# Decoder kernel, layer 0: who issues the rows of maxima, where the raw mask lands, and the order of SyncE's queue

## The chip, the cores and the metric

The kernel runs on one core of one Trainium2 chip. The metric is the device time of one execution in microseconds (us). The engines are TensorE (PE), VectorE (DVE), ScalarE (ACT), GpSimd (POOL) and SyncE (SP); SP computes nothing and issues DMAs. DMAs that an engine issues stand in the profile as SPq or ACTq.

## The reference, cut to what matters

A decoder of four layers, each of self attention, cross attention over a context and a feed-forward part, on x of 4 batches x 256 tokens x 128 features; the context has 4 x 512 tokens. The change lies in layer 0:

```
x = x + L0_attn(layernorm(x))                  # self attention, 16 half heads of 8 features, pairs combined
x = x + L0_xattn(ctx, ctx, layernorm(x), mask) # cross attention, 16 heads of 8 features
x = x + L0_ffn(layernorm(x))                   # 8 experts and a shared one

# L0_attn
probs = softmax(einsum('bhtd,bhsd->bhts', rope(q), rope(k)))     # 256 x 256 per half head
diff  = probs[:, :, 0] - lam * probs[:, :, 1]
attn  = einsum('bhts,bhsd->bhtd', diff, v); attn *= rsqrt(mean(attn*attn) + 1e-5) * (1 - LAMBDA_INIT)
# L0_xattn
energy = einsum('nqhd,nkhd->nhqk', q, k)
energy = where(mask == 0, -1e20, energy)                         # mask: 4 x 1 x 256 x 512, int32
out    = einsum('nhql,nlhd->nqhd', softmax(energy / sqrt(128)), v) @ W_fc.T + b_fc
```

## The kernel before, in words

The kernel is written out by hand: each engine has one program (`tensor_program`, `scalar_program`, `vector_program`, `gpsimd_program`, `sync_program`), run in its own order, and the engines meet only at semaphores. Nothing is reordered by a scheduler.

The two attentions of layer 0 run as one sequence of slots `t` (line 1188). In self attention (A0) a batch has 8 slots, one per pair of heads; cross attention (X0) has 16 slots per batch and begins at slot 36, so that its slot 0 is the same as A0's slot 36. In a slot TensorE makes one pair's scores (L545 for A0, L550 for X0), VectorE takes their maxima (L1666, L1672), and 12 slots later (20 in X0) TensorE makes the transposed scores again with the maximum subtracted (L531), ScalarE takes the exponentials (L1242) and TensorE sums them with the values (L585). Each batch is closed some 21 slots after it began: VectorE and GpSimd normalise it (`l0a_rms`, `power`, L2426), TensorE turns and projects it (L509, L517), and VectorE, GpSimd, TensorE and ScalarE make its X0 queries (`turn_norm`, L478; `split_queries`, L2439 to L2442).

The operands of the scores are stacks: `q_stack` (per batch), `self_stack` (A0's keys) and `ctx_stack` (the context's keys). A float32 operand is split in three bf16 parts, which a DMA writes to DRAM (`write_parts`, L2596, to `q_scr`, `k_scr`, `c_scr`), and which two DMAs (one for each parity of heads) read back into 48 rows of a stack (`fill_rows`, L2602). Further rows of a stack hold ones or zeros (`fill_row`, L2618), and three rows of `q_stack` hold the parts of the row maxima, which come from `mT` (`max_rows`, L2644). TensorE waits for these at the first exponential slot of a batch (`d_maxrow`, L557), for a batch's queries at its first score slot (`d_qfill`, L564) and for the context's stack at X0's slot 0 (`d_cfill`, L680).

SP issues nearly all DMAs, in the order of `sync_program`; an instruction there that waits holds up all behind it. In the first stage the order is: the stacks of batch 0; the transposed context `ctxT` (1 MB); batch 1; the raw mask (2 MB, into `ctx_stack`, which is free then); batch 2; maxima of batch 0; batch 3; the context's parts (12 writes); maxima of batch 1; the bulk loads `rows`, `vaug`, `keep`; maxima of batch 2; then, once GpSimd has turned the raw mask into `far_q` (L2565, `far_done`), the rows and parts of `ctx_stack`; X0's queries of batch 0; maxima of batch 3; X0's other queries and its first maxima; the weights of the feed-forward part (`L0f_w`, 4.6 MB).

GpSimd's order (lines 2551 to 2572) is: keys of batches 0 to 2, context pieces 0 and 1, keys of batch 3, context pieces 2 and 3, the mask (8 instructions), and then for each batch the root (L2426) with which it is closed.

Of the kernel before, what the change touches and what calls it, by code (L numbers as in the profile page):

```python
# [23 lines left out]
ALU = mybir.AluOpType  # L24
# [128 lines left out]
CFILL = {X0: 64, X1: 160, X2: 224}  # L153
# [41 lines left out]
def build(nc, d, out, ctx):  # L195
# [98 lines left out]
    mask_raw = ctx_flat[:, 0:4096].bitcast(I32).rearrange("p (t k) -> p t k", t=NT)  # L294
# [165 lines left out]
    def tensor_program():  # L460
# [216 lines left out]
        def cross_slot(use, t, w_out, following, tile=ring):  # L677
            if t == 0:
                pe.wait_ge(d_ones, 128)
                pe.wait_ge(d_cfill, CFILL[use])  # L680
# [531 lines left out]
    def scalar_program():  # L1212
# [67 lines left out]
        def l0a_slot(t):  # L1280
            g, odd = divmod(t - 15, 2)
            if not odd and 0 <= g < 16:
                lift(A0, g, SUM0[A0] + g + 1)
            for b in range(B):
                at = t - close_slot(A0, b)
                if at == 4:
                    turned_close(A0, b)
                if at == 8:
                    turned_norm("L0x", b, qT, scale=RSQRT128)
            if t == 8:  # L1290
                act.wait_ge(lam_sum, 1)
                act.activation(lam[:, 2:4], lam[:, 0:2], ACT.Exp).then_inc(lam_exp, 1)
            if 0 <= t - 12 < 32:
                exps(A0, t - 12)
            if t == 10:
                l0a_values_of(3)

        def cross_slot(use, t, following):
# [3 lines left out]
            for b in range(B):  # L1302
# [1114 lines left out]
    def gpsimd_program():  # L2417
# [145 lines left out]
        pool.wait_ge(d_raw, 16)  # L2563
        for t in range(NT):
            pool.tensor_scalar(far_q[:, t, :], mask_raw[:, t, :], 0, -BIG, ALU.is_equal, ALU.mult).then_inc(far_done, 1)  # L2565
# [25 lines left out]
    def sync_program():  # L2591
# [100 lines left out]
        for b in range(1, B):  # L2692
            max_rows(X0, b)
# [190 lines left out]
```

## Time and profile before

| | us |
|---|---|
| median of 3 runs (lowest, highest) | 1306.96 (1304.37, 1311.36) |
| the profiled execution's own time | 1301.29 |
| its span | 1300.0 |
| busy PE / DVE / ACT / POOL | 1018.1 / 809.3 / 588.7 / 232.9 |
| DMA queue q1 (SP's) | 65.19 MB, 15.7% of 16 engines' span |

The chain that ended last is 55% PE, 27% DVE, 5% DMA. A share over the whole span says little of one stage, so the stretch from 0 to about 200 us, in which the changed code runs, has to be read by itself: where its engines stood still, and what ended that. In the rows, "idle before <- releaser" is in square brackets, and the engine PEld is TensorE's load of weights.

### The profile page before, as it was taken

The page shows a single profiled execution, that of the slowest core. Times are in us where ns is not written, and L with a number is a line of the kernel's source. Part 1 is how long each engine was busy: PE and PEld are TensorE (multiplying, and loading weights), DVE is VectorE, ACT ScalarE, POOL GpSimd, SP SyncE. Part 2 cuts the span into 40 slices and gives each one's busy share as a digit, 9 for nine tenths or more (in the row PEclk, how much of TensorE's full clock was granted, in tenths as well). Part 3 has the DMA queues.
Part 4 walks back from the last instruction along what each step waited for, and adds up shares of the span by engine and source line. Part 5 has one row for each costly group of instructions (what it writes and reads, how often), then busy time and mean ns, then how long its engine had stood idle before and what let it go on. Part 6 is the DMA issues. An engine that isn't in the chain of part 4 may idle for free.

```text
span 1300.0 us, 18604 instructions
## 1 busy us (share of the span) xinstructions
PE 1018.1 (78%) x7025; PEld 543.5 (42%) x7025; DVE 809.3 (62%) x2015; ACT 588.7 (45%) x975; POOL 232.9 (18%) x299
## 2 busy tenths in 40 slices
PE   3375559999899995586766789999856878868999
PEld 2132212333377673344444233466522333336757
DVE  5575476771221646888777785486778878765422
ACT  1054315666424533687673568422203645533342
POOL 3362230000000023376542100000101100110000
PEclk9587657999789997577777699899956889989999
DMA  4663132000000030044102500310100300100000
GB/s 118 201 246 116 41 95 100 2 2 2 1 1 1 1 98 33 4 143 139 59 1 94 178 3 2 86 51 1 42 7 25 124 1 2 33 1 1 1 9 9
DMA packets 47680, 67.42 MB, mean 52 GB/s; under 512 B 4903, under 2 KB 41976, under 8 KB 45896
## 3 DMA queue, kind: packets, MB, share of 16 engines
q1 hardware_dynamic: 46872, 65.19, 15.7%
q10 hardware_dynamic: 720, 1.05, 0.3%
q8 instruction: 56, 0.92, 0.3%
q14 instruction: 32, 0.26, 0.1%
HBM read 46.83 MB, written 19.01 MB: 51 GB/s over the span
## 4 chain that ended last, share of the span: by engine, by line
PE 55%; DVE 27%; DMA 5%; issue 4%; ACT 4%; SPq 2%; POOL 2%; DVEq 0%; ACTq 0%; POOLq 0%
PE ps_s L755 9%; PE ps_e L745 9%; DVE mx L1676 6%; PE ps_v L585 6%; PE ps_e L531 4%; PE ps_s L550 3%; PE ps_e L529 3%; DMA q_scr<-parts 3%; DVE ps_s L1672 2%; PE ps_e L842 2%; PE ps_s L829 2%; DVE work L2154 2%; ACT work L1242 2%; DVE work L2156 2%; DVE xn L1632 1%
## 5 line engine op out<-in xcount | busy, mean ns | idle before, releaser
L1242 ACT ACTIVATE work<-ps_e 128x512 f32<-128x512 f32 x448 | 250.6, 597 | 185.8 <-PE ps_e L531 180.6
L550 PE MATMUL ps_s<-ctx_stack,q_stack 49*128 49x512 bf16 x384 | 130.9, 466 | 52.5 <-DVE mx L1676 37.5
L1676 DVE TENSOR_REDUCE mx<-ps_s 128x2 f32<-128x1024 f32 x128 | 153.7, 1221 | 29.2 <-PE ps_s L550 27.8
L2426 POOL TENSOR_TENSOR rstd<-rstd,halves 128x2 f32<-128x2 f32 x52 | 36.7, 706 | 751.2 <-DVE rstd L1619 751.1
L1335 ACT ACTIVATE work<-ps_s,keep 128x512 f32<-128x512 f32 x136 | 93.1, 687 | 146.2 <-PE ps_s L755 143.2
L531 PE MATMUL ps_e<-q_stack,ctx_stack 52*128 52x256 bf16 x768 | 149.8, 293 | 12.0 <-DMA q_stack<-mT 4.4
L585 PE MATMUL ps_v<-work,vaug 128*32 128x256 f32 x1536 | 130.0, 414 | 4.6 <-ACT work L1230 4.6
L745 PEld LDWEIGHTS ps_e<-ffn_w,work 128*128 128x128 f32 x960 | 119.2, 198 | 21.0 <-issue 19.9
L755 PE MATMUL ps_s<-xnT,ffn_w 128*128 128x512 f32 x240 | 119.8, 627 | 3.6 <-ACT work L1335 3.6
L745 PE MATMUL ps_e<-ffn_w,work 128*128 128x128 f32 x960 | 121.0, 281 | 0.8 <-DVE x L1870 0.8
L1672 DVE CUSTOM_DVE_ANT_0 ps_s<-ps_s,work 128x512 f32<-128x512 f32 x128 | 85.9, 716 | 56.5 <-PE ps_s L550 56.3
L1880 DVE SCALAR_TENSOR_TENSOR x<-ps_e,gates,x 128x128 f32<-128x128 f32 x128 | 39.0, 346 | 127.0 <-PE ps_e L745 124.0
L531 PEld LDWEIGHTS ps_e<-q_stack,ctx_stack 52*128 52x128 bf16 x768 | 45.0, 96 | 108.2 <-ACT work L1242 50.6
L550 PEld LDWEIGHTS ps_s<-ctx_stack,q_stack 49*128 49x128 bf16 x384 | 29.4, 98 | 81.5 <-DVE mx L1676 51.4
L755 PEld LDWEIGHTS ps_s<-xnT,ffn_w 128*128 128x128 f32 x240 | 42.6, 199 | 45.2 <-issue 25.5
L529 PE MATMUL ps_e<-work,ident_b 128*128 128x512 bf16 x128 | 52.4, 409 | 5.4 <-issue 5.4
L1666 DVE TENSOR_REDUCE mx<-ps_s 128x4 f32<-128x1024 f32 x32 | 38.1, 1218 | 22.1 <-PE ps_s L545 21.8
L585 PEld LDWEIGHTS ps_v<-work,vaug 128*32 128x32 f32 x1536 | 31.6, 111 | 47.9 <-issue 35.5
L2482 POOL TENSOR_TENSOR work<-work 128x1536 f32<-128x1536 f32 x14 | 48.0, 3439 | 12.8 <-ACT work L1473 12.8
L531 PE MATMUL ps_e<-q_stack,self_stack 52*128 52x256 bf16 x128 | 23.4, 333 | 30.4 <-DMA q_stack<-mT 29.6
L1707 DVE RECIPROCAL rsum<-ps_s 128x8 f32<-128x8 f32 x48 | 9.7, 202 | 60.0 <-PE ps_s L501 60.0
L1222 ACT ACTIVATE xnT<-ps_m 128x256 f32<-128x256 f32 x36 | 13.8, 383 | 68.1 <-PE ps_m L478 67.3
(358 smaller groups left out, 1748.2 us busy)
## 6 DMA issues: line engine op xcount, KB each, us to landing
q_stack<-q_scr SPq DMA_DIRECT2D x40, 192.0 KB
ctx_stack<-c_scr SPq DMA_DIRECT2D x4, 1536.0 KB
ffn_w<-in_L0f_w SPq DMA_DIRECT2D x1, 4608.0 KB, 15.2
q_scr<-parts SPq DMA_DIRECT2D x20, 192.0 KB, 2.1
ffn_w<-in_L1f_w SPq DMA_DIRECT2D x1, 3456.0 KB, 14.0
self_stack<-k_scr SPq DMA_DIRECT2D x16, 192.0 KB
ctx_stack<-kx_scr SPq DMA_DIRECT2D x2, 1536.0 KB
ffn_w<-in_L3f_w SPq DMA_DIRECT2D x1, 3072.0 KB, 13.2
```

The lines of the kernel that those rows point to most:

```text
L529: pe.matmul(bank[name], ident_b[:], far_k[:, b, k:k + 2, :].rearrange("p k q -> p (k q)"), start=True, stop=False, skip_group_check=True)
L531: m = pe.matmul(bank[name][:, half * S:(half + 1) * S], stack[p0:p0 + K_EXP, pair, b * nk + k * P:b * nk + (k + 1) * P], q_stack[p0:p0 + K ...
L550: return pe.matmul(ps_s[i][:, parity, :], q_stack[p0:p0 + K_SCORE, b, pair, part * P:(part + 1) * P], ctx_stack[p0:p0 + K_SCORE, pair, b * ...
L585: m = pe.matmul(ps_v[j * COLS:(j + 1) * COLS, 0:S], values(b * nkt + k, g % 4 * GROUP + j), pt[:, j % 2, k % 2, :], start=(k == 0), stop=( ...
L745: m = pe.matmul(bank[name][:, i * P:(i + 1) * P], hid[:, j, (t0 + i) * P:(t0 + i + 1) * P], w2(e, j), start=(j == 0), stop=(j == FJ - 1))
L755: pe.matmul(bank[name], w1_of(st, e, j), xnT[:, g * 512:(g + 1) * 512], start=True, stop=True).then_inc(UPS[st], 1)
L1242: act.activation(pt[:, parity, :, :].rearrange("p k q -> p (k q)"), bank[f"e{parity}"], ACT.Exp).then_inc(exped, 1)
L1335: act.activation(hid_unit(st, u)[:, j, :], bank[f"h{n % 2}"], ACT.Gelu_apprx_tanh, bias=b1).then_inc(HIDS[st], 1)
L1672: m = dve.tensor_tensor_reduce(ps_s[i][:, parity, :], ps_s[i][:, parity, :], far_q[:, b * TPB + part, :], 1.0, -3e38, ALU.add, ALU.max, mx ...
L1676: m = dve.tensor_reduce(mx[:, b, :, pair, part], ps_s[i][:], AX, ALU.max, negate=True)
L1880: m = dve.scalar_tensor_tensor(x[:, t, :], bank[f"e{(n - 1) % 2}"][:, i * P:(i + 1) * P], scalar_of(e, t), x[:, t, :], ALU.mult, ALU.add)
L2482: pool.tensor_tensor(c, c, l1_s[:, HALVES[n], :], ALU.add).then_inc(added, 1)
```

## The change

Six edits, in layer 0's two attentions alone.

- `max_rows` for A0 and X0 is issued by ScalarE, from a new function in `scalar_program`, in A0's slots 11, 19, 27, 35 and in X0's slots 18, 34, 50, 66, ahead of the slot's exponentials. Later stages keep SP's.
- The raw mask is loaded in two halves, into `ffn_w` and into `work`, and no longer into `ctx_stack`.
- The rows of ones of `ctx_stack` are written at the start (on `d_cfill`, whose counts go up by 32).
- SP writes the parts of batches 1 and 2 and fills both stacks ahead of `ctxT` and of the mask.
- `ctx_stack` is filled right behind the context's parts and `rows`, ahead of `keep` and `vaug`; that fill waits for `d_cwrite` alone and no longer for `far_done`.
- X0's queries of all four batches stand in a row, without maxima between them.

```
-        pool.wait_ge(d_raw, 16)
+        pool.wait_ge(d_raw, 32)
...
+        def max_rows(use, b):
+            act.wait_ge(max_T, BATCH0[use] + b + 1)
+            for parity in range(2):
+                p0 = parity * SLOT + ROW_MAX
+                act.dma_start(q_stack[p0:p0 + 3, b, :, :].rearrange("s h (q t) -> s (h q) t", q=TPB),
+                              mT[parity * 48:(parity + 1) * 48, b, :]).then_inc(d_maxrow[b], 16)
...
+            if t in (11, 19, 27, 35):
+                max_rows(A0, (t - 11) // 8)
...
+            if use == X0 and t in (18, 34, 50, 66):
+                max_rows(X0, (t - 18) // 16)
...
+        fill_row(ctx_stack, one_row, 3, ROW_MAX, d_cfill)
         lam_at = ROW_AT["lq1"][0]
         self_attention_inputs(A0, 0)
+        sp.dma_start(rows[:, lam_at:], ...).then_inc(d_lam, 16)
+        for b in (1, 2):
+            queries(A0, b)
+            keys(A0, b)
+        for b in (1, 2):
+            fill_queries(A0, b)
+            fill_self_keys(A0, b)
         sp.dma_start(ctxT, d["ctxT"][:, :]).then_inc(d_ctx, 16)
-        self_attention_inputs(A0, 1)
-        sp.dma_start(rows[:, lam_at:], ...).then_inc(d_lam, 16)
-        sp.dma_start(mask_raw, ...).then_inc(d_raw, 16)
-        self_attention_inputs(A0, 2)
-        max_rows(A0, 0)
+        for half in range(2):
+            sp.dma_start(mask_raw[half], mask_tiles[:, 4 * half:4 * half + 4, :]).then_inc(d_raw, 16)
         self_attention_inputs(A0, 3)
         for g in range(4):
             ...
-        max_rows(A0, 1)
         sp.dma_start(rows[:, 0:lam_at], ...).then_inc(d_rows, 16)
+        sp.wait_ge(d_cwrite, 192)
+        fill_context(c_scr, zero_row)
+        sp.dma_start(keep[:, P:KEEP_N], ...).then_inc(d_keep, 16)
         sp.dma_start(vaug_pad[:, 0:NC * VA], ...).then_inc(d_vload, 16)
-        sp.dma_start(keep[:, P:KEEP_N], ...).then_inc(d_keep, 16)
         ...
-        max_rows(A0, 2)
+        for b in range(B):
+            cross_inputs(X0, b)
         sp.wait_ge(far_done, NT)
-        sp.wait_ge(d_cwrite, 192)
-        fill_row(ctx_stack, one_row, 3, ROW_MAX, d_ones)
-        fill_context(c_scr, zero_row)
-        cross_inputs(X0, 0)
-        max_rows(A0, 3)
-        for b in range(1, B):
-            cross_inputs(X0, b)
-        max_rows(X0, 0)
         sp.wait_ge(x_done, X_AT[A0, B - 1])
         sp.dma_start(ffn_w[:, 0:FFN_N], d["L0f_w"][:, :]).then_inc(d_w, 16)
-        for b in range(1, B):
-            max_rows(X0, b)
```

SP, from the filling of batch 0's stacks to the transposed context; before (`write_parts` is L2596, `fill_rows` L2602, `in_ctxT` the context, `in_mask_L0` the raw mask):

```order
L2602 DMA q_stack<-q_scr 48x1x2048 x2
L2602 DMA self_stack<-k_scr 48x8x256 x2
L2663 DMA work<-in_ctxT 128x2048
L2596 DMA q_scr<-parts 128x3x256
L2596 DMA q_scr<-parts 128x2x256
L2596 DMA q_scr<-parts 128x256
```

SP, the same place of the changed kernel, from the last write of batch 2's keys on (there these functions are L2608 and L2614):

```order
L2608 DMA k_scr<-work 128x256
L2614 DMA q_stack<-q_scr 48x1x2048 x2
L2614 DMA self_stack<-k_scr 48x8x256 x2
L2614 DMA q_stack<-q_scr 48x1x2048 x2
L2614 DMA self_stack<-k_scr 48x8x256 x2
L2683 DMA work<-in_ctxT 128x2048
L2686 DMA ffn_w<-in_mask_L0 128x4x512
L2686 DMA work<-in_mask_L0 128x4x512
```

The context stood behind four fills, those of batch 0; now it stands behind twelve, and behind the 12 writes of batches 1 and 2.

SP, from the context's last write to the first of X0's queries; before (`in_rows01` holds the zeros and ones):

```order
L2596 DMA c_scr<-ffn_w 128x512
L2644 DMA q_stack<-mT 3x16x128 x2
L2674 DMA rows<-in_rows 128x2689
L2675 DMA vaug<-in_v_aug 128x2304
L2676 DMA keep<-in_keep 128x2664
L2677 DMA masku8<-in_mask_keys 16x128
L2678 DMA b2<-in_b2_L0 9x128
L2679 DMA b2<-in_b2_L3 8x128
L2644 DMA q_stack<-mT 3x16x128 x2
L2618 DMA ctx_stack<-in_rows01 3x8x2048 x2
L2602 DMA ctx_stack<-c_scr 48x1x16384 x2
L2618 DMA ctx_stack<-in_rows01 1x8x2048 x2
```

SP, the same place of the changed kernel:

```order
L2608 DMA c_scr<-ffn_w 128x512
L2691 DMA rows<-in_rows 128x2689
L2614 DMA ctx_stack<-c_scr 48x1x16384 x2
L2630 DMA ctx_stack<-in_rows01 1x8x2048 x2
L2694 DMA keep<-in_keep 128x2664
L2695 DMA vaug<-in_v_aug 128x2304
L2696 DMA masku8<-in_mask_keys 16x128
L2697 DMA b2<-in_b2_L0 9x128
L2698 DMA b2<-in_b2_L3 8x128
L2608 DMA q_scr<-parts 128x3x256
```

The fill of `ctx_stack` now stands ahead of `keep` and `vaug`, which X0's queries still follow; no rows of maxima stand between.

ScalarE around A0's slot 27 in the changed kernel (exponentials L1243, sums out of `ps_v` L1231, the new rows of maxima L1259; the queue of before has the same rows without the DMA):

```order
L1243 ACTIVATE work<-ps_e0 128x512
L1243 ACTIVATE work<-ps_e1 128x512
L1231 ACTIVATE work<-ps_v 128x256
L1259 DMA q_stack<-mT 3x16x128 x2
L1243 ACTIVATE work<-ps_e0 128x512
L1243 ACTIVATE work<-ps_e1 128x512
```

The two DMAs stand between a lift and the exponentials of their slot, which they hold up.

## Rows read from the trace of the kernel before

**Rows 1.** Windows: us, busy (x) of PE, PEld, DVE, ACT, POOL; PEclk, DMA share, GB/s

```profile
100.00:120.00 20.00, 14.78 (x155) 6.84 (x147) 16.32 (x49) 12.32 (x26) 7.56 (x10) 0.90 0.42 129
120.00:140.00 20.00, 0.00 (x0) 0.00 (x0) 0.82 (x4) 0.00 (x1) 0.62 (x2) 0.53 0.24 83
```

**Rows 2.** Chain of waits, 100 to 145 us: start, us, what

```profile
108.88 25.00 DMA q_scr<-parts
133.89 0.79 SPq L2602
...
136.31 4.17 DMA q_stack<-mT
```

**Rows 3.** Timeline of TensorE: start, us, line, operation, [idle before <- releaser]

```profile
48.49 1.04 PE L545 MATMUL ps_s<-self_stack,q_stack 49*128 49x256 bf16 x8 [6.13 <-DMA self_stack<-k_scr]
...
64.01 0.39 PE L531 MATMUL ps_e<-q_stack,self_stack 52*128 52x256 bf16 x1 [6.39 <-DMA q_stack<-mT]
...
119.17 0.41 PE L501 MATMUL ps_s<-keep,work 128*128 128x128 f32 x2 [0.28 <-ACT work L1230]
...
140.52 0.61 PE L531 MATMUL ps_e<-q_stack,self_stack 52*128 52x256 bf16 x4 [20.95 <-DMA q_stack<-mT]
...
143.55 0.61 PE L550 MATMUL ps_s<-ctx_stack,q_stack 49*128 49x512 bf16 x2
...
194.18 0.58 PE L529 MATMUL ps_e<-work,ident_b 128*128 128x512 bf16 x1 [5.39 <-issue]
```

**Rows 4.** Timeline of SP's queue: start, us of issue, line, DMA, count

```profile
25.84 3.02 SPq L2663 DMA_DIRECT2D work<-in_ctxT  x1
...
30.92 2.49 SPq L2596 DMA_DIRECT2D k_scr<-work  x3
37.42 1.48 SPq L2602 DMA_DIRECT2D q_stack<-q_scr  x2
...
62.78 1.52 SPq L2596 DMA_DIRECT2D k_scr<-work  x3
...
68.43 9.74 SPq L2596 DMA_DIRECT2D c_scr<-ffn_w  x12
...
99.99 1.58 SPq L2602 DMA_DIRECT2D ctx_stack<-c_scr  x2
...
186.45 1.48 SPq L2602 DMA_DIRECT2D q_stack<-q_scr  x2
187.98 1.57 SPq L2644 DMA_DIRECT2D q_stack<-mT  x2
```

**Rows 5.** Windows again, as rows 1

```profile
40.00:44.00 4.00, 1.32 (x10) 0.27 (x8) 3.96 (x5) 0.00 (x0) 3.59 (x5) 0.50 0.38 131
...
82.00:92.00 10.00, 7.07 (x69) 3.06 (x69) 7.12 (x16) 5.03 (x10) 5.03 (x3) 0.83 0.96 367
...
136.00:139.00 3.00, 0.00 (x0) 0.00 (x0) 0.00 (x0) 0.00 (x0) 0.00 (x0) 0.50 0.33 121
```

**Rows 6.** Timeline of GpSimd

```profile
36.36 0.61 POOL L2439 CAST ffn_w<-work 128x512 bf16<-128x512 f32 x1 [5.83 <-DMA work<-in_ctxT]
...
59.54 0.40 POOL L2439 CAST work<-xn 128x256 bf16<-128x256 f32 x1 [15.72 <-DVE xn L1651]
...
61.84 0.61 POOL L2439 CAST ffn_w<-work 128x512 bf16<-128x512 f32 x1
...
69.38 15.95 POOL L2565 TENSOR_SCALAR work<-ctx_stack 128x512 bf16<-128x512 int32 x8
...
90.21 2.92 POOL L2426 TENSOR_TENSOR l0a_ss<-l0a_ss,halves 128x16 f32<-128x16 f32 x1 [4.89 <-DVE l0a_ss L1741]
```

**Rows 7.** DMAs of the page: KB each, median us from issue to landing

```profile
c_scr<-ffn_w SPq DMA_DIRECT2D x4, 384.0 KB, 3.6
```

**Rows 8.** Timelines of VectorE and ScalarE

```profile
187.57 0.21 DVE L1696 COPY mT<-ps_s 96x128 bf16<-96x128 bf16 x1
...
235.79 1.27 ACT L1242 ACTIVATE work<-ps_e 128x512 f32<-128x512 f32 x2 [0.59 <-PE ps_e L531]
```

More of the change, by code:

```diff
@@ L152 @@
 LAST = {A0: 54, X0: 96, X1: 96, X2: 93, "chain": 125}
-CFILL = {X0: 64, X1: 160, X2: 224}
+CFILL = {X0: 96, X1: 192, X2: 256}
 QKV_N = 3 * E + 1
@@ L293, in build @@
     ctx_flat = ctx_stack[:].rearrange("p h t -> p (h t)").bitcast(F32)
-    mask_raw = ctx_flat[:, 0:4096].bitcast(I32).rearrange("p (t k) -> p t k", t=NT)
+    mask_raw = [part.bitcast(I32).rearrange("p (t k) -> p t k", t=NT // 2)
+                for part in (ffn_w[:, ROOM_AT + 3072:ROOM_AT + 5120], wk(4096, 2048))]
     far_q = wk(0, 2048).bitcast(BF16).rearrange("p (t k) -> p t k", t=NT)
@@ L678, in cross_slot @@
             if t == 0:
-                pe.wait_ge(d_ones, 128)
+                pe.wait_ge(d_ones, 96)
                 pe.wait_ge(d_cfill, CFILL[use])
@@ L2562, in gpsimd_program @@
         split_context(3)
-        pool.wait_ge(d_raw, 16)
+        pool.wait_ge(d_raw, 32)
         for t in range(NT):
-            pool.tensor_scalar(far_q[:, t, :], mask_raw[:, t, :], 0, -BIG, ALU.is_equal, ALU.mult).then_inc(far_done, 1)
+            pool.tensor_scalar(far_q[:, t, :], mask_raw[t // 4][:, t % 4, :], 0, -BIG, ALU.is_equal, ALU.mult).then_inc(far_done, 1)
         pool.wait_ge(d_rows, 16)
@@ L2660, in sync_program @@
         fill_row(self_stack, zero_row, 1, ROW_MASK, d_ones)
+        fill_row(ctx_stack, one_row, 3, ROW_MAX, d_cfill)
         lam_at = ROW_AT["lq1"][0]
         self_attention_inputs(A0, 0)
-        sp.dma_start(ctxT, d["ctxT"][:, :]).then_inc(d_ctx, 16)
-        self_attention_inputs(A0, 1)
-        sp.dma_start(rows[:, lam_at:], d["rows"][0:1, lam_at:].broadcast_to([P, ROW_N - lam_at])).then_inc(d_lam, 16)
-        sp.dma_start(mask_raw, d["mask_L0"].rearrange("b o (j p) k -> p (b o j) k", p=P)).then_inc(d_raw, 16)
-        self_attention_inputs(A0, 2)
-        max_rows(A0, 0)
+        sp.dma_start(rows[:, lam_at:], d["rows"][0:1, lam_at:].broadcast_to([P, ROW_N - lam_at])).then_inc(d_lam, 16)
+        for b in (1, 2):
[4 more added lines that the diff above has]
+            fill_self_keys(A0, b)
+        sp.dma_start(ctxT, d["ctxT"][:, :]).then_inc(d_ctx, 16)
+        mask_tiles = d["mask_L0"].rearrange("b o (j p) k -> p (b o j) k", p=P)
+        for half in range(2):
+            sp.dma_start(mask_raw[half], mask_tiles[:, 4 * half:4 * half + 4, :]).then_inc(d_raw, 16)
         self_attention_inputs(A0, 3)
@@ L2672, in sync_program @@
             write_parts(c_scr, KEY_PARTS, c_parts[:, :, g * 512:(g + 1) * 512], g * 512, 512, d_cwrite)
-        max_rows(A0, 1)
         sp.dma_start(rows[:, 0:lam_at], d["rows"][0:1, 0:lam_at].broadcast_to([P, lam_at])).then_inc(d_rows, 16)
+        sp.wait_ge(d_cwrite, 192)
+        fill_context(c_scr, zero_row)
+        sp.dma_start(keep[:, P:KEEP_N], d["keep"][:, P:KEEP_N]).then_inc(d_keep, 16)
         sp.dma_start(vaug_pad[:, 0:NC * VA], d["v_aug"][:, :]).then_inc(d_vload, 16)
-        sp.dma_start(keep[:, P:KEEP_N], d["keep"][:, P:KEEP_N]).then_inc(d_keep, 16)
         sp.dma_start(masku8[:], d["mask_keys"].rearrange("b (j p) -> (b j) p", p=P)).then_inc(d_mk, 16)
```

## The prediction

> **What bounds the kernel now.** I read the windows of 20 us first, to see where TensorE stands still though it has work. From 120 to 140 us every compute engine is idle and the DMA engines are busy for 0.24 of their time [rows 1]. The chain of waits for that stretch says why: a DMA that writes query parts takes 25.00 us to land, SP then issues the fill of `q_stack` at 133.89, and behind it the rows of maxima take 4.17 us [rows 2]. TensorE's timeline gives the price: 20.95 us before its first exponential of A0's batch 3, and X0's first score follows at 143.55 [rows 3]. So the first stage ends in one stall of 21 us, and all that follows in this in-order kernel starts from it. Two more waits on the same kind of rows stand in that timeline: 6.39 us at 64.01 (batch 0) and 5.39 us at 194.18, which is marked "issue" but lies between the issue of X0's rows at 187.98 and their landing [rows 3, 4].
>
> Why did 64 KB take 25 us? They were issued at 108.88 behind the fill of `ctx_stack`, issued from 99.99 on [rows 4]. While only fills are in flight, the share of busy DMA engines is 0.38 or 0.33 [rows 5], which is about 6 of 16. I take it that one fill, whatever its size, runs on six engines, and that what SP issues later waits behind it there. The fill takes about 101.6 to 133.9 = 32.3 us.
>
> **The sum.** It is a new timeline of SP's queue and of what it waits for, against the profiled execution (1301.29 us, 1.29 of them around its span).
>
> *Batches 1 and 2.* A batch's two query fills and two key fills took 37.42 to 48.49 = 11.1 us from first issue to TensorE's use [rows 3, 4], some 9.4 of them on the engines. Before, batch 1's fills stood behind its writes and 1 MB of context. Now `rows` (16.5 KB) takes the context's place, the writes of batch 1 again end at about 33.4 [rows 4], those of batch 2 at about 37, and batch 1's fills land at about 37 + 10 = 47: batch 1 starts 1.5 us sooner. Batch 2's follow 9 us later, at about 56.
>
> *The transposed context* comes behind them: 56 + 2 = 58 us, where GpSimd had it at 36.36 [rows 6]. GpSimd's queue then is: two pieces of context 7.5 us (as 61.84 to 69.38), batch 3's keys 2.3 (59.54 to 61.84), two more pieces 7.5, and the mask 15.95 [rows 6]. That gives 58 + 7.5 + 2.3 + 7.5 + 15.95 = 91.2 us for the root that closes batch 0, which now starts at 90.21 after an idle 4.89 [rows 6]. So the slack in GpSimd's queue is used up, and A0 passes its slot 24 no sooner than before. What TensorE gains at batch 1, and in the wait of 6.39 us at batch 0's maxima, it gives back there. I count 0 for both; their bounds are the 8 us of these two and a loss of as much if the context comes later.
>
> *The context's stack.* Batch 3's keys are split at 58 + 7.5 + 2.3 = 67.8; their three writes take 1.5 to issue [rows 4] and some 2.5 to land (a context write of twice the size takes 3.6 [rows 7]), two fills 1.6: 73.5. The 12 writes of the context take 9.74 us of issue [rows 4] and land 3.6 later: SP's wait ends, and the fill is issued, at about 87, against 99.99. It is 13 us sooner, because neither the mask on GpSimd nor maxima of batch 2 hold it. The data follow the 1.3 MB of `rows`, so say from 88.6, and 32.3 us later, at 120.9, the fill is in. But `keep` and `vaug` now stand behind it: of the 3.9 MB (`rows`, `vaug` and `keep` by their shapes) that moved in the 10 us of 82 to 92 [rows 5] they are 2.5 MB, or 6.5 us. X0's query parts, ready near 108 as now, land at 127.9 (now 133.89), and the fill of `q_stack` takes about 5.4 us (with the rows of maxima behind it 133.89 to 140.52 = 6.6, of which I give these 1.2): X0's first score is at about 133.3. Slots 24 to 35 go as before, since maxima no longer queue at SP, and slot 36's own A0 work (3.0 us between 140.52 and 143.55 [rows 3]) is done before the wait. Gain: 143.55 - 133.3 = **10.2 us**. Bounds: 16.8 if `keep` and `vaug` cost nothing there; 3.7 if they cost twice that.
>
> *X0's rows of maxima, batch 0.* VectorE has them at 187.57 + 0.21 [rows 8] and SP issues at 187.98, so issuing elsewhere saves no wait; but the DMAs land 194.18 - 189.55 = 4.6 us after issue, behind a fill issued at 186.45 [rows 4]. On ScalarE's own queue they need not stand behind it. Bounds 0 and 4.6, I take **2.4 us**.
>
> *ScalarE's issue.* SP pays 1.57 us for two such DMAs [rows 4]. In A0 this delays the exponentials of slots 27 and 35, and the rows share engines with the fill of `ctx_stack`; but between slot 35 (119.2) and 133.3 there are 14 us of stall that hide it. X0's batch 0 finds ScalarE idle. For X0's batches 1 to 3 ScalarE waits only 0.59 us between pairs [rows 8], so each is late by 1.57 - 0.59 = 1.0 us: at most 3 us where TensorE waits for each, 0 where the two banks take it up; I take **1.5 us** lost. Later in the kernel nothing is touched.
>
> The mask in two halves, the earlier rows of ones and X0's queries in a row I cost at nothing: what they move is covered by the stall. Without that cover the ones (192 KB at the 367 GB/s of [rows 5]) would add 0.5 us before the first projection.
>
> Sum: -10.2 - 2.4 + 1.5 = -11.1: 1290.2 us by the profiled execution. That one lies 5.7 us under the median of the runs shown, 1306.96; by that median it is 1295.9. I predict **1296 us**.
>
> *A rule of the Trainium skill against it.* The page "DMA: Bandwidth & Descriptors" (section "Issuing engines are not separate DMA queues") says that DMAs of SP, ScalarE and GpSimd run on the same 16 engines and interleave, and that issuing from several only saves issue time. By it the 2.4 us fall away, since the issue wait was 0.2 us here. The same page (section "Queues, rings and completion order") lets an engine alternate between the queues by packets, by which the rows would pass most of a fill. No row of this trace shows two busy queues; that is why the term stands at the middle of its bounds.
>
> **Rivals.**
>
> *Larger gain.* The context is in sooner, or `keep` and `vaug` slip in on the ten idle engines and cost the six little. For it: 0.24 of DMA share from 120 to 140 means that the fill's engines end unevenly. The first score is at 126.5, a gain of 16.8 + 2.4 - 1.5 = 17.7: 1289 us by the median. Chance 0.16.
>
> *The stall stays where it is.* `keep` and `vaug` cost 13 us behind the fill instead of 6.5: the score at 139.8, with the other terms a gain of 4.6: 1302. For it: with `rows` they needed 10 us on all engines at a share of 0.96 [rows 5]. Against it: fills leave ten engines free. Chance 0.19.
>
> *The rows of maxima gain nothing on ScalarE's queue.* The issue wait it could save is 187.98 - 187.78 = 0.2 us, and if on the DMA engines the rows still follow the fill of 186.45, they land as now: -10.2 + 1.5 = -8.7: 1298. Chance 0.10. The Trainium skill's section on issuing engines, above, describes this case.
>
> *Slower: the transposed context starves GpSimd.* It waits behind eight fills more, and GpSimd can't go on to batch 3's keys without it. For it: SP's issue already takes 3.02 us where it stands behind four fills [rows 4]. Every us that the context lands after 58 moves batch 3, the 12 writes, the context's stack and A0's slot 24 by one. It decides from 58 + 11 = 69 us on. If eight fills take twice their time, it lands at about 76 + 2: 9 us slower, 1316. Chance 0.13.
>
> **How the numbers follow.** My forecast (gain of 7 to 15) has 0.42. Less than 0.5% (6.5 us) can't be told from no change here. Faster by more: 0.40 of the forecast, 0.06 of the rows that gain nothing, 0.16 of the larger gain, 0.02 of the stall that stays = 0.64. Within: 0.02 + 0.04 + 0.16 + 0.04 = 0.26. Slower by more: 0.01 + 0.09 = 0.10. The range goes from 1284, a gain of 23 (the larger gain and the first stage's 8 us kept in part), to 1307, no gain.
>
> **What would show it.** Right: GpSimd's first context piece starts at 55 to 61 us and its first root (on `l0a_ss`) at 89 to 95 with little idle; `ctx_stack` is filled from 84 to 90; the last part of X0's first queries lands at 125 to 131; TensorE's stall is now ahead of a score (L551), 10 to 15 us long, and ends near 133; the rows of maxima land within 3 us of their issue on ScalarE's queue at X0's slot 20; the stretch from there to the end is as long as before. Wrong: the context after 65 us, the fill of `ctx_stack` after 93, TensorE waiting for rows of maxima in A0 for more than some us, or a new wait behind ScalarE's issue in X0's slots 34, 50 and 66.

## The result: 2.0% slower, and the profile after

| | before | after |
|---|---|---|
| median, us (lowest to highest, runs) | 1305.66 (1298.46 to 1311.36, 4) | 1332.19 (1329.26 to 1334.08, 4) |
| profiled execution's own time | 1301.29 | 1331.33 |
| its span | 1300.0 | 1330.0 |
| TensorE's mean granted clock | 0.848 | 0.829 |

The ratio is 1.0204, with a 95% interval of 1.0149 to 1.0259. The forecast was 1296, its range 1284 to 1307, and 0.10 for slower: wrong in sign.

Where the 30.0 us of span came in, TensorE's timeline shows (start, us, what, [idle before <- releaser]); the columns answer to [rows 3].

```profile
44.13 1.04 PE L546 MATMUL ps_s<-self_stack,q_stack 49*128 49x256 bf16 x8 [4.64 <-DMA self_stack<-k_scr]
...
57.94 0.39 PE L532 MATMUL ps_e<-q_stack,self_stack 52*128 52x256 bf16 x1 [4.92 <-DMA q_stack<-mT]
...
81.49 0.39 PE L532 MATMUL ps_e<-q_stack,self_stack 52*128 52x256 bf16 x1 [4.89 <-DMA q_stack<-mT]
...
130.35 0.39 PE L532 MATMUL ps_e<-q_stack,self_stack 52*128 52x256 bf16 x1 [29.45 <-DMA q_stack<-mT]
...
154.43 0.61 PE L551 MATMUL ps_s<-ctx_stack,q_stack 49*128 49x512 bf16 x2
...
217.82 0.39 PE L532 MATMUL ps_e<-q_stack,ctx_stack 52*128 52x256 bf16 x1 [16.80 <-issue]
...
367.14 1.20 PE L756 MATMUL ps_s<-xnT,ffn_w 128*128 128x512 f32 x1
```

Batch 1 starts 4.4 us sooner (44.13 for 48.49), and batch 0's rows of maxima 6.1 us sooner. Then come two waits that the forecast did not have. The first is 29.45 us at slot 28, for the rows of maxima of A0's batch 2. It swallows the old stall of 20.95 us and more: X0's first score starts at 154.43, 10.9 us later than before, where the forecast had 133.3. The second is 16.80 us at X0's first exponential, where 5.39 stood before; the stretch from X0's first score to that row grew from 50.6 to 63.4 us, so by 12.8. From that row to the first GELU operand of the feed-forward part (L756) it takes 149.32 us, against 150.20 before (194.18 to 344.38). So the stretch up to there is longer by 10.9 + 12.8 - 0.9 = 22.8 us, of 30.0 in all. The other 7.2 lie in code that is the same in both kernels (962.9 us from L756 to the end for 955.6). The eleven experiments below, with that same code, have 958.5 to 967.7 us there, so I take these 7.2 as scatter of the stretch, in which the profile of before was the shortest of all. TensorE's granted clock in it was 0.87 before and 0.85 after. The medians, 26.5 us apart, leave only 3.7 us for it. What makes it scatter, and whether the change has a part in it, was not tested.

The chain of waits (start, us, what) names the first stall as [rows 2] named the old one.

```profile
99.97 0.38 ACT work L1231
100.35 0.38 ACTq L1259
100.77 29.54 DMA q_stack<-mT
...
203.35 14.47 issue
```

ScalarE issues the rows at 99.97, and they take 29.54 us from issue to landing. That is not a wait to issue; it is a transfer of 24 KB in flight. SP's queue (start, us of issue, what) says what was in flight with it; it answers to [rows 4].

```profile
43.30 3.16 SPq L2683 DMA_DIRECT2D work<-in_ctxT  x1
...
67.93 10.13 SPq L2608 DMA_DIRECT2D c_scr<-ffn_w  x12
...
82.22 1.48 SPq L2614 DMA_DIRECT2D ctx_stack<-c_scr  x2
...
85.17 0.44 SPq L2694 DMA_DIRECT2D keep<-in_keep  x1
85.65 0.43 SPq L2695 DMA_DIRECT2D vaug<-in_v_aug  x1
...
136.74 1.71 SPq L2608 DMA_DIRECT2D q_scr<-parts  x3
139.99 1.56 SPq L2614 DMA_DIRECT2D q_stack<-q_scr  x2
...
200.26 0.39 SPq L2703 DMA_DIRECT2D ffn_w<-in_L0f_w  x1
```

The fill of `ctx_stack` goes out at 82.22, 17.8 us sooner than before and so ahead of the rows of batch 2. Right behind it on SP's queue come the bulk loads `keep` (1332 KB) and `vaug` (1152 KB), 85.17 and 85.65. Before, the order of SP's queue kept the fill behind the rows: `max_rows(A0, 2)` at 97.23, then the fill at 99.99 [rows 4]. Likewise `L0f_w` (4608 KB) is issued at 200.26, 0.2 us after X0's rows, while SP before issued it behind them on the same queue (189.59, the rows at 187.98). The two lines of SP's old queue that [rows 4] leaves out:

```profile
97.23 1.47 SPq L2644 DMA_DIRECT2D q_stack<-mT  x2
...
189.59 0.43 SPq L2691 DMA_DIRECT2D ffn_w<-in_L0f_w  x1
```

ScalarE's timeline has the two sets of rows beside them, and one of those in X0's later batches:

```profile
99.97 1.53 ACTq L1259 DMA_DIRECT2D q_stack<-mT  x2
...
200.04 1.50 ACTq L1259 DMA_DIRECT2D q_stack<-mT  x2
...
250.35 1.08 ACT L1243 ACTIVATE work<-ps_e 128x512 f32<-128x512 f32 x2 [2.48 <-PE ps_v L586]
```

What the DMA engines do in the first stall, the windows show (columns as [rows 1]):

```profile
100.00:120.00 20.00, 0.85 (x10) 0.35 (x6) 2.73 (x9) 1.44 (x3) 0.86 (x2) 0.57 0.37 99
120.00:140.00 20.00, 9.28 (x69) 3.67 (x69) 5.78 (x11) 4.77 (x10) 3.54 (x5) 0.50 0.19 62
```

and the view of DMA queues shows who gets through (q1 is SP's, q10 ScalarE's; packets, MB, share of 16 engines), in the windows 106 to 114, 114 to 122, 122 to 130, and for the second wait 204 to 212 and 212 to 219:

```profile
q1 hardware_dynamic: 28, 0.79, 35.5%
q10 hardware_dynamic: 16, 0.00, 0.3%
...
q1 hardware_dynamic: 63, 0.74, 35.6%
q10 hardware_dynamic: 28, 0.01, 0.5%
...
q1 hardware_dynamic: 119, 0.65, 20.1%
q10 hardware_dynamic: 57, 0.01, 0.8%
...
q1 hardware_dynamic: 92, 3.14, 98.5%
q10 hardware_dynamic: 14, 0.00, 0.2%
...
q1 hardware_dynamic: 47, 1.14, 38.2%
q10 hardware_dynamic: 88, 0.02, 1.4%
```

In the first window 28 packets of SP's queue carry 0.79 MB; by the trace 24 of them are the fill's, of 32 KB each, and such a packet takes 1.2 to 2.6 us. In the same 8 us 16 packets of the rows get through, which would hardly occupy one engine. All three windows together carry 101 of the rows' 102 packets (96 of 256 B and 6 of 4 B). So ScalarE's rows do pass the fill, but only by a small packet now and then.

The wait does not end with the fill alone. In the second and third window SP's packets are smaller on average (12 and 5 KB): the packets of `keep` (10.7 KB) and `vaug` (9.2 KB) have their turn. The fill's last packet ends at 122.8, with 50 of the rows' 96 through; the last packet of `vaug` ends at 129.5, and the rows' last starts in that same moment. If nothing had followed the fill, the rows could have landed some 6 us sooner; that is my estimate from these times. In the second stall the last packet of `L0f_w` ends at 216.3, and 46 of the 96 packets of rows go after it.

GpSimd's timeline answers to [rows 6] and went much as forecast:

```profile
53.53 0.61 POOL L2451 CAST ffn_w<-work 128x512 bf16<-128x512 f32 x1 [23.42 <-DMA work<-in_ctxT]
...
88.93 2.92 POOL L2438 TENSOR_TENSOR l0a_ss<-l0a_ss,halves 128x16 f32<-128x16 f32 x1 [2.04 <-DVE l0a_ss L1753]
```

### The profile page after: what moved, and what is told of

Read it like the earlier page. It is cut to its first block, busy times and chain, and to the rows that moved or that the text cites. A ratio compares the mean times of both kernels' runs of the same rounds, so it can differ in the third digit from the quotient of the medians.

```text
span 1330.0 us, 18586 instructions
## 1 busy us (share of the span) xinstructions
PE 1025.6 (77%) x7006; PEld 549.1 (41%) x7025; DVE 817.1 (61%) x2015; ACT 588.7 (44%) x975; POOL 233.0 (18%) x299
## 4 chain that ended last, share of the span: by engine, by line
PE 55%; DVE 27%; DMA 5%; issue 5%; ACT 4%; SPq 1%; POOL 1%; ACTq 0%; DVEq 0%; POOLq 0%
PE ps_s L756 9%; PE ps_e L746 9%; PE ps_v L586 6%; DVE mx L1688 6%; PE ps_e L532 5%; DMA q_stack<-mT 4%; PE ps_s L551 3%; PE ps_e L530 2%; DVE ps_s L1684 2%; PE ps_e L843 2%; PE ps_s L830 2%; ACT work L1243 2%; DVE work L2166 2%; DVE work L2168 2%; DVE xn L1644 1%
## 5 line engine op out<-in xcount | busy, mean ns | idle before, releaser
L1243 ACT ACTIVATE work<-ps_e 128x512 f32<-128x512 f32 x448 | 250.3, 597 | 209.8 <-PE ps_e L532 196.4
L1347 ACT ACTIVATE work<-ps_s,keep 128x512 f32<-128x512 f32 x136 | 93.0, 687 | 148.3 <-PE ps_s L756 145.5
L756 PE MATMUL ps_s<-xnT,ffn_w 128*128 128x512 f32 x240 | 121.7, 635 | 3.6 <-ACT work L1347 3.6
L746 PE MATMUL ps_e<-ffn_w,work 128*128 128x128 f32 x960 | 120.9, 281 | 0.8 <-DVE x L1882 0.8
L756 PEld LDWEIGHTS ps_s<-xnT,ffn_w 128*128 128x128 f32 x240 | 43.4, 202 | 46.1 <-issue 26.1
L532 PE MATMUL ps_e<-q_stack,self_stack 52*128 52x256 bf16 x128 | 26.7, 362 | 41.7 <-DMA q_stack<-mT 41.2
L1644 DVE TENSOR_SCALAR xn<-x,mv,rstd 128x128 f32<-128x128 f32 x96 | 38.1, 443 | 14.3 <-POOL rstd L2438 14.3
L530 PE MATMUL ps_e<-work,ident_b 128*128 128x512 bf16 x109 | 44.2, 406 | 1.6 <-ACT work L1243 1.6
```

What stands on the lines that cost most here:

```text
L530: pe.matmul(bank[name], ident_b[:], far_k[:, b, k:k + 2, :].rearrange("p k q -> p (k q)"), start=True, stop=False, skip_group_check=True)
L532: m = pe.matmul(bank[name][:, half * S:(half + 1) * S], stack[p0:p0 + K_EXP, pair, b * nk + k * P:b * nk + (k + 1) * P], q_stack[p0:p0 + K ...
L746: m = pe.matmul(bank[name][:, i * P:(i + 1) * P], hid[:, j, (t0 + i) * P:(t0 + i + 1) * P], w2(e, j), start=(j == 0), stop=(j == FJ - 1))
L756: pe.matmul(bank[name], w1_of(st, e, j), xnT[:, g * 512:(g + 1) * 512], start=True, stop=True).then_inc(UPS[st], 1)
L1243: act.activation(pt[:, parity, :, :].rearrange("p k q -> p (k q)"), bank[f"e{parity}"], ACT.Exp).then_inc(exped, 1)
L1347: act.activation(hid_unit(st, u)[:, j, :], bank[f"h{n % 2}"], ACT.Gelu_apprx_tanh, bias=b1).then_inc(HIDS[st], 1)
```

## The experiments

Theory A: the loss is two small transfers (rows of maxima: 256 B to a packet) that now fly beside large ones with large packets, the fill of `ctx_stack` (with `keep` and `vaug` behind it) at slot 28 and `L0f_w` in X0. Against it stand a slow issue on ScalarE, the queue itself, and the new order of batches 1 and 2. All kernels but e4 and e9 are the changed kernel with the edit shown. The kernel before was run again beside each group of experiments, and each ratio is to it: its median was 1304.60 us beside e1, e2, e3 and e5, 1301.53 beside e4, e6, e9 and e10, and 1303.47 beside e11, e12 and e14.

**e1: the fill in small packets.** The same bytes in eight DMAs, cut by columns:

```
-            fill_rows(c_scr, ctx_stack[:], d_cfill)      # 2 DMAs, runs of 32 KB
+            for g in range(4):                           # 8 DMAs, runs of 1 KB
+                for parity in range(2):
+                    sp.dma_start(ctx_stack[p0:p0 + ROW_MASK, :, g * 512:(g + 1) * 512], scr...[:, :, :, g * 512:(g + 1) * 512])
```

> Change: the context stack is filled at the same place of SP's queue, but in 8 DMAs of runs of 1 KB instead of 2 DMAs of runs of 32 KB. Theory A (the rows of maxima on ScalarE's queue go by one small packet per packet of the fill, 32 of them on each engine that carries them, and a packet of the fill is about 26 KB and 0.9 us): TensorE's wait of 29.4 us before A0's exponentials of batch 2 falls under 6 us, while X0's wait of 16.8 us behind the feed-forward weights stays; the kernel is 10 to 25 us faster than the changed one, near 1310 to 1320. Rival B (rows wait until everything that SP issued earlier has landed, whatever its packets): the wait of 29 us stays or grows, since the fill is no shorter; 1330 or more.

Measured: 1307.97 us (10 runs), ratio to before 1.0013 (0.9979 to 1.0048). Its TensorE timeline:

```profile
114.70 0.39 PE L532 MATMUL ps_e<-q_stack,self_stack 52*128 52x256 bf16 x1 [8.62 <-DMA q_stack<-mT]
...
139.18 0.61 PE L551 MATMUL ps_s<-ctx_stack,q_stack 49*128 49x512 bf16 x2
...
198.13 0.59 PE L530 MATMUL ps_e<-work,ident_b 128*128 128x512 bf16 x1 [16.63 <-issue]
```

The first wait falls from 29.45 to 8.62 us (I had expected under 6), and X0's first score comes 15.3 us sooner. The second wait, to which nothing was done, stays. The edit changed two things, though. The same bytes of the fill fly on the same queue in smaller packets; but SP needs 19.68 us to issue the eight DMAs, so that `keep` and `vaug` go out at 105.50 and 106.71, behind the rows (104.62) and no longer ahead of them.

**e2: the weights behind the rows.**

```
+        sp.wait_ge(d_maxrow[0], 64)
         sp.dma_start(ffn_w[:, 0:FFN_N], d["L0f_w"][:, :]).then_inc(d_w, 16)
```

> Change: SP waits until X0's rows of maxima of batch 0 have landed before it issues the 4.6 MB of feed-forward weights. Theory A: the 16.8 us before X0's first exponential fall to 2 to 4 us, nothing else moves: 12 to 14 us faster than the changed kernel, near 1319. Rival C (that wait is due to the fill of batch 3's queries issued 1.4 us before): it stays above 4 us, with at most 12 us gained, and the rest of the wait ends when those fills land.

Measured: 1313.26 us (5 runs), ratio 1.0082 (1.0054 to 1.0109).

```profile
130.27 0.39 PE L532 MATMUL ps_e<-q_stack,self_stack 52*128 52x256 bf16 x1 [23.42 <-DMA q_stack<-mT]
...
200.93 0.58 PE L530 MATMUL ps_e<-work,ident_b 128*128 128x512 bf16 x1 [4.01 <-issue]
```

Now the second wait goes (4.01) and the first stays. It ends at 130.27, to 0.1 us where it ended in the changed kernel, and again as the last packet of `vaug` ends (129.2). TensorE came to it 6 us later here, so the end says more than the length. By the two ratios (1.0204 and 1.0082) the kernel gained some 16 us, where I had expected 12 to 14.

**e3: the fill behind batch 2's rows.**

```
-        sp.wait_ge(d_cwrite, 192)
-        fill_context(c_scr, zero_row)          # ahead of keep and vaug
...
+        sp.wait_ge(d_cwrite, 192)
+        sp.wait_ge(d_maxrow[2], 32)
+        fill_context(c_scr, zero_row)          # ahead of X0's queries
```

> Change: the context stack is filled only after the rows of maxima of A0's batch 2 have landed (near 100 us, where the kernel before issued it); all else as in the changed kernel. Theory A: TensorE's wait at A0's batch 2 (29.4 us) goes; the fill (103 to 135 us) now meets the rows of batch 3, so that TensorE waits some 20 us at slot 36 and X0 starts at 138 to 143, as before the change; 8 to 14 us faster than the changed kernel. Rival D (ScalarE as issuer is slow by itself, without a fill in flight): a wait of more than 5 us at batch 2 stays.

Measured: 1326.12 us (5 runs), ratio 1.0170 (1.0131 to 1.0210).

```profile
89.62 0.39 PE L532 MATMUL ps_e<-q_stack,self_stack 52*128 52x256 bf16 x1 [10.20 <-DMA q_stack<-mT]
...
150.24 0.61 PE L532 MATMUL ps_e<-q_stack,self_stack 52*128 52x256 bf16 x4 [20.73 <-DMA q_stack<-mT]
```

The wait at slot 28 is gone (2.15 us at 111.22), so ScalarE's issue is not slow by itself. But the stall has only moved to batch 3's rows, which now meet the fill issued at 111.25, and batch 1's meet `keep` and `vaug`. X0's first score at 157.32 is later than the 138 to 143 that I had expected, and the gain on the changed kernel is 6 us by the medians in place of 8 to 14: moving a large transfer does not remove the collision while rows fall due every 24 us.

**e5: all rows back on SP, the early fill kept.**

```
-            if t in (11, 19, 27, 35): max_rows(A0, (t - 11) // 8)        # ScalarE
-            if use == X0 and t in (18, 34, 50, 66): max_rows(X0, (t - 18) // 16)
+        max_rows(A0, 2)                        # SP, behind keep and vaug; X0's first ahead of L0f_w
```

> Change: the changed kernel with all rows of maxima back on SP (batch 2's behind keep, vaug and the small loads), the early fill kept. Theory A with first in, first out on SP's own queue: the rows of batch 2 land when the fill, keep and vaug have, near 125 us, so that a wait of 22 to 28 us at A0's slot 28 stays, but X0's rows land ahead of the feed-forward weights and that wait falls from 16.8 to 5 or 6 us: 10 to 16 us faster than the changed kernel. Rival D (the issuing queue is the cause): the wait at slot 28 is under 8 us and the kernel is as fast as before the change or faster.

Measured: 1315.66 us (4 runs), ratio 1.0094 (1.0059 to 1.0130).

```profile
133.87 0.39 PE L532 MATMUL ps_e<-q_stack,self_stack 52*128 52x256 bf16 x1 [28.71 <-DMA q_stack<-mT]
...
205.82 0.59 PE L530 MATMUL ps_e<-work,ident_b 128*128 128x512 bf16 x1 [4.51 <-issue]
```

The rows, issued at 100.06 behind the bulk on SP's own queue, land at 133.87, 3.5 us later than beside it on ScalarE's. But SP issued the fill 3.1 us later here (85.35 for 82.22), since it had rows of batches 0 and 1 to issue as well, and the last packet of `vaug` ends 2.9 us later (132.4 for 129.5). So ScalarE's queue is worth about half a us here, and the early fill with the two loads behind it causes the stall on either queue. X0's wait is short, since SP's order again keeps `L0f_w` behind the rows.

**e4: the kernel before, with ScalarE's issue alone.** The order of the rest, and the mask's place, are the old ones.

```
+            if t in (11, 19, 27, 35):                            # ScalarE
+                max_rows(A0, (t - 11) // 8)
+            if use == X0 and t in (18, 34, 50, 66):
+                max_rows(X0, (t - 18) // 16)
-        max_rows(A0, 0) ... max_rows(X0, 3)                      # SP: all eight gone
```

> The kernel before with one part of the change alone: ScalarE issues the rows of maxima of A0 and X0; the order of the other DMAs is the old one, the mask lies where it lay. SyncE no longer waits for VectorE's maxima of batch 2, so the context's fill moves by itself to the end of the mask on GpSimd, about 86 us, and L0f_w no longer stands behind X0's rows. Theory A: both losses of the changed kernel appear here too. TensorE waits 20 to 30 us at slot 28, 10 to 17 us at X0's slot 20, and the time is 1318 to 1332. Rival E (the loss comes from the new order of batches 1 and 2 and of the mask): slot 28 waits under 5 us, and the time is 1300 to 1308.

Measured: 1312.88 us (6 runs), ratio 1.0084 (1.0052 to 1.0115).

```profile
93.13 0.39 PE L531 MATMUL ps_e<-q_stack,self_stack 52*128 52x256 bf16 x1 [14.79 <-DMA q_stack<-mT]
...
117.37 0.40 PE L531 MATMUL ps_e<-q_stack,self_stack 52*128 52x256 bf16 x1 [4.83 <-DMA q_stack<-mT]
...
200.26 0.39 PE L531 MATMUL ps_e<-q_stack,ctx_stack 52*128 52x256 bf16 x1 [16.82 <-issue]
```

Theory A was right on the second wait (16.82) and wrong on the slot of the first: batch 1's rows were caught, not batch 2's. ScalarE issued them at 77.17, in the same moments as SP issued `rows`, `vaug` and `keep` (76.48 to 79.08), which stood behind those rows in SP's old order. TensorE was so late then that batch 2's rows (111.60) met only the fill's end. The wait went to whichever rows met the large transfers. The time lies under the 1318 to 1332 that I had expected.

**e9: the kernel before, with the new order of batches 1 and 2 and of the mask alone.** SP keeps the rows of maxima and the late fill.

```
         self_attention_inputs(A0, 0)
+        for b in (1, 2): queries(A0, b); keys(A0, b)
+        for b in (1, 2): fill_queries(A0, b); fill_self_keys(A0, b)
         sp.dma_start(ctxT, ...)
+        for half in range(2): sp.dma_start(mask_raw[half], ...)  # ffn_w and work
         max_rows(A0, 0)
```

> The kernel before with the other part alone: stacks of batches 1 and 2 ahead of the transposed context and the mask, and the mask in two halves in ffn_w and work; SyncE issues the rows of maxima where it did, and the context's fill stays behind the maxima of batch 2. Theory A: batch 1 starts some 4 us sooner (44 for 48.5), GpSimd's first root starts at 89 to 92 as in the changed kernel, the stall of 21 us ahead of the rows of batch 3 stays, since the order there is the old one, and X0's first score comes 0 to 5 us sooner: 1300 to 1305 us. Rival E (the new order is a part of the loss): X0's first score later than 145 us and the time above 1309.

Measured: 1301.76 us (12 runs), ratio 1.0016 (0.9996 to 1.0037), no change. Batch 1 starts at 44.48, the old stall is there (15.47 us before 139.35), and X0's first score comes at 142.38, 1.2 us sooner. This part is harmless and, as measured, almost useless.

**e6: both mends, e1 and e2 together.**

> The changed kernel with both mends at once: the context's fill in eight DMAs with runs of 1 KB, and SyncE waiting for the rows of maxima of X0's batch 0 ahead of L0f_w. Theory A (the loss is two transfers of small packets that stand behind big packets, once in A0's batch 2 and once in X0's batch 0, and nothing else): the two mends add up. TensorE's wait at slot 28 stays at about 9 us, X0's wait falls from 16.6 to about 4, X0's first score comes at about 139: 1308.0 - 12.6 = about 1295 us (1292 to 1300), which is under both kernels. Rival B (there is a further loss in the change, somewhere after layer 0's attentions, of the 7 us that the profiled execution showed there): the two waits go as said, but the time stays at 1300 or above.

Measured: 1296.20 us (12 runs), ratio 0.9950 (0.9926 to 0.9974): faster than both kernels.

```profile
108.01 0.39 PE L532 MATMUL ps_e<-q_stack,self_stack 52*128 52x256 bf16 x1 [6.68 <-DMA q_stack<-mT]
...
132.33 0.61 PE L551 MATMUL ps_s<-ctx_stack,q_stack 49*128 49x512 bf16 x2 [1.38 <-DMA q_stack<-q_scr]
...
180.59 0.39 PE L532 MATMUL ps_e<-q_stack,ctx_stack 52*128 52x256 bf16 x1 [3.99 <-issue]
```

The two mends add up, and nothing of the loss is left. X0's first score at 132.33 is near where the forecast had put it for the change as it was (133.3).

This run also shows the role of the packets most directly. From 100 to 108 us SP's queue carries the fill alone, in packets of 1 KB:

```profile
q1 hardware_dynamic: 915, 0.92, 37.2%
q10 hardware_dynamic: 102, 0.02, 1.5%
```

All 102 packets of the rows get through in these 8 us, where 16 did beside the 32 KB packets of the changed kernel, from 106 to 114 us, at nearly the same share of the DMA engines (35.5%).

**e11 and e12: the size of the packets.** To separate packet size from the number of DMAs, e6 with the fill cut by heads: eight DMAs with runs of 8 KB, or four with 16 KB.

```
-                    sp.dma_start(ctx_stack[p0:p0 + ROW_MASK, :, g * 512:(g + 1) * 512], scr...
+                    sp.dma_start(ctx_stack[p0:p0 + ROW_MASK, g * 2:(g + 1) * 2, :], scr...     # e12: 4 for 2
```

> The kernel with both mends, but the context's eight fills cut by heads instead of by columns: two heads each, so that a run is 8 KB where it was 1 KB; as many DMAs, as many bytes, the same queues. Theory A (each small packet of the rows waits for one packet of the fill on its engine, so the wait grows with the size of the fill's packets): between 6.7 us (1 KB, the kernel with both mends) and 23.4 us (32 KB, the kernel with the weights behind the rows), in proportion: TensorE waits 6.7 + (23.4 - 6.7) x 8 / 32 = about 11 us at slot 28 (9 to 14), the time is 1297 to 1303. Rival F (what helped was that eight DMAs are issued one after the other and let the rows in between, whatever their packets): 6 to 8 us as with both mends, the time 1293 to 1298.

> As the kernel with runs of 8 KB, but four fills of four heads each: runs of 16 KB. Theory A: TensorE waits 6.7 + (23.4 - 6.7) x 16 / 32 = about 15 us at slot 28 (13 to 18), the time is 1301 to 1308. Rival F (the number of DMAs counts): 6 to 10 us, 1293 to 1300.

Measured: 1306.57 us (10 runs), ratio 1.0021 (0.9994 to 1.0048), and 1314.60 (8 runs), ratio 1.0089 (1.0063 to 1.0115). The row at slot 28, of e11:

```profile
122.90 0.39 PE L532 MATMUL ps_e<-q_stack,self_stack 52*128 52x256 bf16 x1 [15.54 <-DMA q_stack<-mT]
```

and of e12:

```profile
132.07 0.39 PE L532 MATMUL ps_e<-q_stack,self_stack 52*128 52x256 bf16 x1 [23.99 <-DMA q_stack<-mT]
```

With as many DMAs as e6, e11 waits 15.54 us for 6.68, so the number of DMAs by itself is not what helped. The wait grows with the packet: 6.7, 15.5, 24.0, 23.4 us for 1, 8, 16 and 32 KB (the last is e2's). I had expected proportion (11 and 15). It is steeper, and flat from 16 KB on. There the rows land at 130 to 132 us whatever the packet, because the bulk has run out: in e12 the fill ends at 124.6, `vaug` at 131.4, and the rows' last packet starts at 131.4. In e11 they are through at 121.9, ahead of the end of `vaug` (126.0). One thing is not kept apart: in e6 SP is held up while it issues eight fills of 1 KB runs (22.02 us from 84.73; 5.87 us in e11), so `keep` and `vaug` go at 110.28 in e6, behind the rows' landing, and at 90.29 in e11. So the step from 1 to 8 KB is partly theirs: in e10 below, with runs of 1 KB but these two loads ahead of the rows, the wait is 11.38 us. The step from 8 to 16 KB has no such doubt, and neither have the counts of packets under e6.

**e10 and e14: the context in halves.** e6 with pieces 0 and 1 written and filled around batch 3's inputs, pieces 2 and 3 as before; e14 also holds back `keep` and `vaug`:

```
+        context_parts((0, 1))
         self_attention_inputs(A0, 3)
+        sp.wait_ge(d_cwrite, 96)
+        fill_context_pieces(c_scr, (0, 1))
+        context_parts((2, 3))
...
+        sp.wait_ge(d_maxrow[2], 32)            # e14 only
         sp.dma_start(keep[:, P:KEEP_N], ...)
```

> The kernel with both mends, and the context filled in two halves: pieces 0 and 1 are written ahead of batch 3's inputs and filled right behind them, pieces 2 and 3 as before. So less of the fill is left when the rows of maxima of A0's batch 2 are issued near 100 us. Theory A: the wait at slot 28 falls from some 8.6 us to 2 to 6, that at slot 20 (7.2 us, rows issued at about 76) stays or grows by 1 to 3, since the first half is then in flight; together 2 to 5 us sooner than the kernel with both mends: 1290 to 1294. Rival C (what is left of these waits is contention with keep, vaug and rows, not with the fill): the two waits together stay at 14 to 17 us, and the time stays within 2 us of the kernel with both mends.

> The kernel with the context in halves, with one wait more: SyncE lets keep and vaug go only when the rows of maxima of A0's batch 2 have landed. There they were issued at 103.84 and 104.73, in the same moments as those rows (108.28), and TensorE waited 11.38 us. Theory C (what the halves lost is these two loads in flight, not the fill): the wait at slot 28 falls from 11.4 to under 7 us, X0's first score comes at 132 to 138 instead of 145.0, and the time is 1294 to 1300. Rival (the halves themselves cost it, by backpressure on SyncE and batch 3's inputs): the wait stays above 9 us, the time above 1303.

Measured: e10 1307.41 us (12 runs), ratio 1.0037 (1.0013 to 1.0062); e14 1295.50 (10 runs), ratio 0.9930 (0.9898 to 0.9961). The row at slot 28, of e10:

```profile
120.81 0.39 PE L532 MATMUL ps_e<-q_stack,self_stack 52*128 52x256 bf16 x1 [11.38 <-DMA q_stack<-mT]
```

and of e14:

```profile
110.66 0.30 PE L532 MATMUL ps_e<-q_stack,self_stack 52*128 52x256 bf16 x1 [2.71 <-DMA q_stack<-mT]
```

e10 was a miss: half of the fill was out of the way, and the wait grew, because `keep` and `vaug` (packets of some 10 KB) went out at 103.84 and 104.73 and the rows at 108.28. One wait for the rows ahead of them takes 12 us off the median, and e14 came as expected. e14 and e6 are not told apart by their intervals; both beat the kernel before.

## Why the prediction was wrong

**The new timeline of SP was right in the main.** Everything came 2 to 5 us before its forecast, and so a little before the ranges given as signs: the transposed context reached GpSimd at 53.53 (58 forecast, range 55 to 61), the first root started at 88.93 after 2.04 idle (91.2, range 89 to 95), the fill was issued at 82.22 (87, range 84 to 90). The rival in which the context starves GpSimd did not occur. Batch 1 came 4.4 us sooner, not 1.5. "I count 0" for the gains of the first stage holds (e9: 1.2 us at X0's first score). The sum has a slip of 0.5 us: 120.9 + 6.5 is 127.4, not 127.9.

**The term of -10.2 us failed at one step:** "Slots 24 to 35 go as before, since maxima no longer queue at SP". They no longer queued at SP, but they shared the DMA engines. The paragraph on ScalarE's issue named it, "the rows share engines with the fill of `ctx_stack`", and priced it at nothing: "between slot 35 (119.2) and 133.3 there are 14 us of stall that hide it". That cover would hide a delay of batch 3's rows. The rows that met the fill were batch 2's, needed at slot 28 near 101 us, before any stall. Cover there was none, and TensorE waited 29.45 us. The check that was missing: take the new time of issue of every large transfer and its flight (87 to about 121 by my own sum, with 2.5 MB of `keep` and `vaug` behind it), and ask which rows fall due in it. The old fill did not touch batch 2's rows for a reason that stood in the old order, `max_rows(A0, 2)` ahead of the fill. I read that order as a delay that the change removes; it was also a guard.

**The term of -2.4 us** (X0's rows) had the wrong neighbour. I set the rows against the fill of 186.45. The diff also takes `max_rows(X0, 0)` from ahead of `L0f_w`, and 4.6 MB meet the rows: 16.80 us for 5.39, an error of 13.8 with the gain that I had taken. e2 gives it back with one wait.

**The term of +1.5 us** (ScalarE's issue in X0) is neither refuted nor shown. The two profiles, 149.32 for 150.20 us over that stretch, would make it 0 or less. But the three kernels in which SP issues X0's rows (before, e5, e9) have 148.3 to 150.2 us there, mean 149.05, and the ten in which ScalarE does have 149.3 to 152.0, mean 150.92: a difference of about the size forecast.

**The rule weighed against the change.** The wait inside a queue is known from [rows 2]; new is the wait across two queues: 16 small packets in 8 us beside 24 of 32 KB. The Trainium skill, "DMA: Bandwidth & Descriptors", section "Queues, rings and completion order", lets an engine take a packet from each queue in turn. From it I drew that the rows "would pass most of a fill". The trace agrees with the rule, in kind (both queues move packets in the same windows), and not with what I drew: where queues take turns, each small packet pays with the time of large ones, and e6, e11 and e12 show how the price goes with the size. The trace agrees too with the Trainium skill's section "Issuing engines are not separate DMA queues" of that page (the same engines, only issue time saved): by e5 the second queue gains about half a us of 29.

**The forecast's number came true in e6** (1296.20 us, first score 132.33), once the rows no longer met large packets, but partly by luck. The forecast counted 11.1 us down from a median of 1306.96; beside e6 the kernel before had 1301.53, so that e6 gains 5.3 us (0.26% to 0.74%), about half of what was foreseen. The changed kernel lost that, and 26.5 us more in the medians, at two collisions. Shown by the runs are the two causes (each mend takes away or shortens one wait and leaves the other, and both together remove the loss) and that the size of the bulk's packets matters. How much of e1's gain is due to the size, and how much to `keep` and `vaug` held back by it, is not separated. How the DMA engines share out the rows is only argued, and the scatter of the unchanged rest was not pursued.

## What to carry to other kernels

When a queue's order is loosened, list what each instruction stood ahead of as well as what it stood behind: a small, urgent transfer issued first is protected from the bulk behind it, and loses this when another engine issues it. In this kernel a small transfer of many short packets that had to land soon could not stand a transfer with long packets in flight, on either queue. Hold the bulk load until it has landed (e2, e14), but check what it meets then: the fill held back in e3 met the next rows. Or cut the bulk into runs of about 1 KB (e1), and see what the longer issue holds back. Here each of e1, e2 and e14 was worth over 10 us. And list all the bulk in flight, not only the first piece: the wait at slot 28 ended with `vaug`, 7 us after the fill.

## What the runs showed of the hardware that was not expected

- A second queue hardly frees a small transfer: 24 KB in 256 B packets took 29.5 us beside a fill with packets of 32 KB and two loads with packets of about 10 KB. On the same queue behind them (e5) it landed 3.5 us later, of which some 3 us are the later issue of the bulk itself.
- Cutting 3 MB into runs of 1 KB instead of 32 KB went with a shorter wait of the others (29.45 or 23.4 to 8.6 or 6.7 us) and did not make the fill itself slower: from first to last packet it took 27.6 us in e1 and 30.9 in e6, and 30.4 in the kernel before with 32 KB runs (38.6 in the changed kernel, beside `keep` and `vaug`). Its price is SP, which is held for 19.7 to 22.0 us while it issues eight such DMAs, where two of 32 KB runs took 1.48 us. Here that hold-up probably helped, since it kept `keep` and `vaug` back (compare e10 and e14).
